# Moving u*B to GpSimd in 152 of 576 scan steps of a bidirectional Mamba kernel

## The reference

```
xz = u @ W_in; x, z = split(xz); x = silu(conv(x) + b)
dt, B, C = split(x @ W_x);  delta = softplus(dt @ W_dt + b_dt);  A = -exp(A_log)
h[d, n] = exp(delta[d] * A[d, n]) * h[d, n] + delta[d] * x[d] * B[n]      # over time
y[d]    = sum over n of h[d, n] * C[n]
out     = ((y + x * D) * silu(z)) @ W_out
```

## Time and profile before

| what | value |
|---|---|
| median of 3 runs | 2344.05 us (2339.93 to 2344.3) |
| the profiled execution's own time | 2339.7 us |
| its span | 2337.9 us |
| DVE busy | 2127.7 us (91%) |
| PE busy | 1875.8 us (80%) |
| POOL busy | 1613.1 us (69%) |
| ACT busy | 1147.4 us (49%) |

### The profile page before, as it was taken

One profiled execution on the slowest core, in us unless ns is written; L12 is line 12 of the kernel. 1 busy time (PEld: TensorE's weight loads), 2 busy tenths in 40 slices (PEclk: granted clock), 3 DMA queues, 4 the chain that ended last, 5 costly groups with the idle time before them and its releaser, 6 DMA issues. The chain is left out here.

```text
span 2337.9 us, 15732 instructions
## 1 busy us (share of the span) xinstructions
PE 1875.8 (80%) x4794; PEld 723.8 (31%) x4794; DVE 2127.7 (91%) x1429; ACT 1147.4 (49%) x1316; POOL 1613.1 (69%) x704
## 2 busy tenths in 40 slices
PE   5698879787798788788779779869778978877676
PEld 2233333232233233233233323323323323222222
DVE  2899999778999998998999998999899999899996
ACT  3647464644646444534655544644474553353331
POOL 0767875745876884775796686687487678478665
PEclk8899999899999999999999999999999999999999
DMA  3335434333544544443453453454344454345443
GB/s 100 121 139 131 148 141 130 109 104 130 142 144 145 143 145 128 141 149 110 146 159 138 143 152 129 146 142 146 109 140 146 143 143 145 113 151 153 146 149 87
DMA packets 96159, 317.20 MB, mean 136 GB/s; under 512 B 14588, under 2 KB 18956, under 8 KB 95948
## 3 DMA queue, kind: packets, MB, share of 16 engines
q1 hardware_dynamic: 96076, 316.21, 43.2%
HBM read 307.31 MB, written 4.72 MB: 133 GB/s over the span
## 5 line engine op out<-in xcount | busy, mean ns | idle before, releaser
L823 POOL TENSOR_TENSOR ring<-ring,c_ring 128x1024 f32<-128x1024 f32 x576 | 1353.3, 2356 | 644.4 <-DVE ring L769 643.6
L769 DVE TENSOR_TENSOR_SCAN ring<-a_ring,b_ps 128x1024 f32<-128x1024 f32 x576 | 1314.9, 2283 | 37.7 <-issue 0.9
L453 PE MATMUL y_ps<-ring,wp 128*128 128x512 f32 x2304 | 1182.7, 615 | 58.5 <-DVE yv_rows L755 25.6
L453 PEld LDWEIGHTS y_ps<-ring,wp 128*128 128x128 f32 x2304 | 441.6, 196 | 460.1 <-issue 323.7
L573 ACT ACTIVATE a_ring<-delta_ab,neg_a 128x1024 f32<-128x1024 f32 x384 | 435.1, 1144 | 264.1 <-DVE ring L769 258.6
L741 DVE TENSOR_TENSOR b_ps<-u_ab,b_ps 128x1024 f32<-128x1024 f32 x384 | 464.5, 1210 | 102.8 <-PE b_ps L445 79.0
L445 PE MATMUL b_ps<-b_in,sel 96*128 96x512 bf16 x768 | 238.5, 393 | 146.8 <-DVE ring L769 146.5
L573 ACT ACTIVATE a_ring<-delta_m,neg_a 128x1024 f32<-128x1024 f32 x192 | 219.3, 1147 | 265.5 <-DVE ring L769 265.5
L445 PE MATMUL b_ps<-b_in,sel_m 96*128 96x512 bf16 x384 | 119.8, 394 | 148.4 <-DVE ring L769 148.4
L741 DVE TENSOR_TENSOR b_ps<-u_m,b_ps 128x1024 f32<-128x1024 f32 x192 | 232.0, 1208 | 5.0 <-PE b_ps L445 4.7
L500 PE MATMUL bank<-x,w_conv 96*128 96x512 f32 (+12 forms) x576 | 207.2, 602 | 8.3 <-DVE xs L785 8.3
(11 more groups left out here) (82 smaller groups left out, 1095.9 us busy)
## 6 DMA issues: line engine op xcount, KB each, us to landing
c_ring<-c_rows SPq DMA_DIRECT2D x384, 512.0 KB, 3.7
c_ring<-c_rows SPq DMA_DIRECT2D x384, 256.0 KB, 3.9
out<-io SPq DMA_DIRECT2D x16, 192.0 KB, 2.2
io<-x SPq DMA_DIRECT2D x6, 384.0 KB, 4.7
b_in<-parts SPq DMA_DIRECT2D x36, 64.0 KB, 2.1
dt_in<-parts SPq DMA_DIRECT2D x72, 24.0 KB
c_rows<-c_out SPq DMA_DIRECT2D x24, 64.0 KB, 3.2
wp<-wpack SPq DMA_DIRECT2D x1, 1185.0 KB
```

The source lines that it names most:

```text
L453: nc.tensor.matmul(half(y_ps[:, :], j), ident, half(ring[:, g % RING, :], j), start=(n == 0), stop=(n == NS - 1)).then_inc(g_summed, 1)
L769: nc.vector.tensor_tensor_scan(out=h, data0=a, data1=b, initial=0.0, op0=ALU.mult, op1=ALU.add).then_inc(h_ready, 1)
L823: nc.gpsimd.tensor_tensor(r, r, c_ring[:, g % C_RING, :], ALU.mult).then_inc(g_ready, 1)
```

## The change

`BY_POOL` names steps within an item: 11 in `rows`, 13 in `fwd`, 14 in `bwd`, which gives 4 x 38 = 152 steps. In these steps PE spreads no B row and DVE makes no product. SP instead fetches the row B[n] from DRAM, broadcast to 128 partitions, into the new `b_ring` (2 slots in SBUF), up to six steps ahead, and POOL multiplies it in place by u, three steps ahead. The scan of such a step reads a from `a_ring` and b from `b_ring`. ACT's copy that cut out the C rows now takes the B rows too, and SP stores both to DRAM. The slots of `b_ps` go round over the 424 other steps. Smaller packed weights make room for `b_ring`; the products made with them have the same sizes. `ring` keeps its five slots.

```diff
+B_RING = 2
+B_LEAD = 6
+BY_POOL = {ROWS: (2, 8, 13, 17, 19, 23, 26, 30, 31, 37, 47),
+           FWD: (3, 7, 9, 11, 13, 15, 16, 17, 20, 25, 27, 31, 42),
+           BWD: (5, 7, 10, 11, 15, 16, 19, 21, 23, 27, 31, 33, 41, 43)}
-SP_ORDER = ("ahead_c", "jobs")
+SP_ORDER = ("ahead_b", "ahead_c", "jobs")
+POOL_ORDER = ("ahead_b", "product", "jobs")
...
+            def spread_row(dst, rows, k, n, landed_in):
+                if k < 2:
+                    sp.dma_start(dst, rows[k, n:n + 1, :].to_broadcast([P, T])).then_inc(landed_in, 16)
+                    return
+                for b in range(2):
+                    sp.dma_start(dst[b * DM:(b + 1) * DM, :],
+                                 rows[b, n:n + 1, :].to_broadcast([DM, T])).then_inc(landed_in, 16)
...
+            def look_ahead_b(g):
+                if g >= ALL_STEPS:
+                    return
+                kind, pair, k, n = step_at(g)
+                if g % STEPS == 0:
+                    sp.wait_ge(c_kept, 64 * (g // STEPS + 1))
+                if by_pool[g]:
+                    m = pool_before[g]
+                    if m >= B_RING:
+                        sp.wait_ge(h_ready, pool_steps[m - B_RING] + 1)
+                    spread_row(b_ring[:, b_slot(g), :], b_rows[parity(kind, pair)], k, n, b_spread[b_slot(g)])
...
-                wait(pe, h_ready, g - 1)
+                if by_pool[g]:
+                    return
+                m = dve_before[g]
+                if m >= 2:
+                    pe.wait_ge(h_ready, dve_steps[m - 2] + 1)
...
             def scan(g):
...
+                if by_pool[g]:
+                    dve.wait_ge(b_made, pool_before[g] + 1)
+                    b = b_ring[:, b_slot(g), :]
+                else:
+                    dve.wait_ge(b_used, dve_before[g] + 1)
+                    b = b_ps[:, p_slot(g), :]
...
+            def look_ahead(g):
+                if g >= ALL_STEPS or not by_pool[g]:
+                    return
+                kind, pair, k, n = step_at(g)
+                pool.wait_ge(K["set_ready"][kind], 3 * pair + nth(k))
+                pool.wait_ge(b_spread[b_slot(g)], b_uses[g])
+                b = b_ring[:, b_slot(g), :]
+                nc.gpsimd.tensor_tensor(b, u_of(kind, pair, k), b, ALU.mult).then_inc(b_made, 1)
```

More of the change, by code:

```diff
@@ L1 @@
+import itertools
 import numpy as np
@@ L295, in build_program @@
         unit_of = {j[:4]: j[4] for p in PARTS for slot in p["slots"] for j in slot}
+        by_pool = [g % STEPS in BY_POOL[ITEMS[g // STEPS]["kind"]] for g in range(ALL_STEPS)]
+        pool_steps = [g for g in range(ALL_STEPS) if by_pool[g]]
+        dve_steps = [g for g in range(ALL_STEPS) if not by_pool[g]]
+        pool_before = list(itertools.accumulate([0] + [int(x) for x in by_pool]))
+        dve_before = [g - n for g, n in enumerate(pool_before)]
+        dmas = lambda g: 2 if g % STEPS // NS == 2 else 1
         c_uses, spread = [], [0] * C_RING
         for g in range(ALL_STEPS):
-            spread[g % C_RING] += 2 if g % STEPS // NS == 2 else 1
+            spread[g % C_RING] += dmas(g)
             c_uses.append(16 * spread[g % C_RING])
+        b_uses, spread = {}, [0] * B_RING
+        for m, g in enumerate(pool_steps):
+            spread[m % B_RING] += dmas(g)
+            b_uses[g] = 16 * spread[m % B_RING]
+        b_slot = lambda g: pool_before[g] % B_RING
+        p_slot = lambda g: dve_before[g] % 2
         use_of = {j[:4]: j[5] for p in PARTS for slot in p["slots"] for j in slot}
@@ L337, in step_at, with walk @@
             return it["kind"], it["pair"], s // NS, s % NS
-        def walk(order, job, **phases):
+        def walk(order, job, LEAD=LEAD, **phases):
             for n, part in enumerate(PARTS):
@@ L442, in look_ahead @@
                     pe.wait_ge(K["bc_loaded"][kind], BC_LOADS * (pair + 1))
-                wait(pe, h_ready, g - 1)
+                if by_pool[g]:
[3 more added lines that the diff above has]
+                    pe.wait_ge(h_ready, dve_steps[m - 2] + 1)
                 for j in range(2):
-                    last = nc.tensor.matmul(half(b_ps[:, g % 2, :], j), pick(k, n), half(b_in[:, parity(kind, pair), :], j), start=True, stop=True)
+                    last = nc.tensor.matmul(half(b_ps[:, p_slot(g), :], j), pick(k, n), half(b_in[:, parity(kind, pair), :], j), start=True, stop=True)
                 last.then_inc(b_ready, 1)
@@ L525, in job @@
                     src = source(kind, pair)
-                    w = by_batch("w_z", layer, C)
+                    w = col("w_z", layer)[0:C, :]
                     if k < 2:
-                        product(unit, P, [(w[0], half(src[:, k, :], j))])
+                        product(unit, P, [(w[:, 0:P], half(src[:, k, :], j))])
                     else:
-                        product(unit, P, [(w[1 + b], half(src[:, b, :], j)) for b in range(2)])
+                        room(unit)
+                        for b in range(2):
+                            last = nc.tensor.matmul(bank[b * DM:(b + 1) * DM, unit % 2, :], w[:, P:DI], half(src[:, b, :], j),
+                                                    start=True, stop=True)
+                        last.then_inc(produced[unit % 2], 1)
                 elif name == "constants":
@@ L545, in job @@
                     pe.wait_ge(gated_done[kind], 3 * (pair + 1))
-                    w = by_batch("w_out", layer)
-                    product(unit, C, [(w[0], half(yv_of(kind, pair, k), j)), (w[1 + k], half(yv_of(kind, pair, 2), j))])
+                    w, own = col("w_out", layer), slice(k * DM, (k + 1) * DM)
+                    product(unit, C, [(w[:, 0:C], half(yv_of(kind, pair, k), j)),
+                                      (w[own, C:2 * C], half(yv_of(kind, pair, 2), j)[own, :])])
                 elif name == "centre":
@@ L628, in job @@
                     src = full(unit)
-                    if k < 2:
-                        wait(act, b_used, STEPS * (ordinal[kind, pair] - 1) + NS * (k + 1))
+                    if k < 2 and ordinal[kind, pair]:
+                        upto = STEPS * (ordinal[kind, pair] - 1) + NS * (k + 1)
+                        act.wait_ge(b_used, dve_before[upto])
+                        wait(act, b_made, pool_before[upto])
                     bias = sm[:, m_of(k), 5:6]
@@ L850, in tile_of @@
                 return TILES * ordinal[kind, pair]
-            walk(("product", "jobs"), job, product=product)
+            walk(POOL_ORDER, job, ahead_b=look_ahead, product=product)
 def pack(inputs):
```

61 lines of the change are left out of this document (29 added, 32 removed).

## The result

The changed kernel takes 2485.11 us (median of 4 runs, 2481.93 to 2488.66) against 2342.81 us before (4 runs, 2339.93 to 2344.3). The ratio is 1.061, with a 95% interval of 1.0591 to 1.0628: 6% slower, where 5% was forecast.

The account below looks back on a forecast made before the run. DVE was taken to set the pace, with PE as busy in fwd and bwd steps 0 to 17. Forecast: 2339.7 + 85 - 34 + 33 + 30 = 2454, rounded to 2455 us, 5% slower; range 2330 to 2590.

Parts of the forecast that it names:

- The scan waits for POOL: In the 152 moved steps, a scan with two SBUF inputs stands still until the running POOL product has ended.
- POOL waits for the scan: In moved steps, POOL is held while the scan reads two SBUF inputs, taken as 2.09 us per scan.
- The sum by stretch: Per stretch of an item, the longer of POOL's need and the shortened old length: +85 us, corrected by -34.
- the two further waits: Scans meeting a running product in DVE-paced stretches, 33 us, and POOL standing for B rows in fwd, 30 us.
- The waits at DVE's pace: In stretches left to DVE's pace, a scan waits on average half of a running POOL product: 33 us.
- POOL keeps what it holds: Rival: queued POOL products pass a waiting scan, 5 to 7 us on a third of 152; 2585 us or more; 5%.
- my case: Main forecast: moved scans and POOL products exclude each other, the second comer waiting; slower, 2361 to 2585 us, 77%.
- SP's late B rows: In fwd, B rows of steps 16 and 17 delay queued C rows; POOL stands 3.7 us twice per item, 30 us.
- DVE alone waiting: Rival: POOL runs on while a moved scan reads, only DVE waits; 2266 to 2364 us, 10%.
- no contention at all: Rival: moved scans slip between POOL's reads and keep 2.28 us; about 2190 us, faster; 7%.
- The signs named beforehand: Expected in the later profile: scan and POOL product durations, POOL's busy share, DVE's idle waits, middle windows near 60 us.

Follow-up runs that it names:

- The fifth experiment: The changed kernel with 20 of the 152 moved steps given back to PE and DVE: 2415.61 us, ratio to before 1.031.
- the third experiment: The changed kernel, but in the 152 steps ACT writes a to PSUM and the scan reads b from b_ring: 2236.6 us, ratio to before 0.955.

## Why the prediction was right, and which terms were off

**The scan waits for POOL.** Right, and shown by both directions of test: taking the second SBUF operand away takes 250 us off, adding it alone costs 131 us. The row of L800 was enough to read it.

**POOL waits for the scan.** Right: the value 2.09 us was chosen without a row, and the trace shows 2.15 us for the scan's own part, with products held for one DVE instruction and once for four. POOL was held 205 us in all, not 152 x 2.09 = 318: only 93 of its instructions were held by about 2 us, the others met no such scan.

**The sum by stretch.** This is the term with the wrong sizes. It says +10.1 for bwd (10.9 measured), +10.4 for fwd (15.4) and +0.7 for rows (11.9). Inside the items it is off more: the middle stretches (fwd, bwd, rows) were to grow by 7.3, 6.9 and 6.5 us and changed by -4.2, +4.5 and +1.1, while the heads were to change by +4.3, -0.3 and -4.8 and changed by +12.3, +3.1 and +8.7, and the tails by -1.2, +3.5 and -1.0 and changed by +7.3, +3.4 and +2.1. Two things explain part of it. I counted a u*B product in the stretch of its step, but it stands three steps ahead; and the POOL jobs of slot 31 run at the edge, so they fall to the tail: the stretches of fwd 1 have 32, 17 and 29 POOL instructions, where I counted 29, 22 and 23. The head of rows holds the 11-us scan of step 2, which the sum had no term for. Over the twelve items, this sum (+51) and the two further waits (33 and 30) came to +114 us, and 140 were measured; by the sum alone the four `rows` were to change by 3 us and the four fwd by 12, and they changed by 59 and 37. That 2455 lies only 30 us from 2485 is therefore in part luck: stretches forecast too long offset stretches forecast too short.

**The waits at DVE's pace.** 33 us, as if a scan met the rest of one product. It was too small. The rival "POOL keeps what it holds", at 5%, is how the long scans come about, though on some 25 of the 152 and not on a third; most of the others came in at the end of the running product, as my case had it. The fifth experiment puts 70 us on 20 steps.

**SP's late B rows.** 30 us taken, within 0 to 60. POOL stood 14.5 us for them in the changed kernel and 54 us once nothing else held it [group L889 of the third experiment]. The mechanism is there; it is mostly covered here.

**The rivals on the other side.** DVE alone waiting is ruled out by POOL's durations, no contention at all by 3947 against 2283 ns. What the second would have brought, 2190 us, is 46 us below the time with one operand in PSUM, 2236.

**The signs named beforehand.** Scans from PSUM at 2.28 us: yes. POOL's product mean over 2.6: yes, 2.65, but with its maximum at 9.2 instead of 4.5. DVE idle for b: yes, 11.5 us; for `g_summed`, no row. Missed: the mean of the moved scans, 3.95 us instead of 3 to 3.5; POOL over 90% busy, 88%; the middle windows of bwd and rows near 60 us, 57.5 and 54.5.

Open: how much of the loss in the heads, where PE shares the pace, comes from PE itself. The granted clock in the head of fwd 1 is 0.87 where it was 0.96, and the y_ps matmuls take 665 ns on average, 631 in the third experiment. Over the program PE has 119 us less to do and is busy for 58 us longer (1934.1 against 1875.8). No run holds its clock apart from the waits. Open too: why POOL passes a waiting scan in some meetings and not in others that look the same.

## What to carry to other kernels

Before giving DVE's work to POOL, look at where DVE's operands end up, not only at how much POOL has to spare: an instruction that reads PSUM and SBUF and one that reads SBUF twice have the same duration alone and not beside a busy POOL. One slow instance of a similar instruction in the trace (maximum twice the median, its end tied to another engine's end) is enough to expect the halts. It does not give their number: the moved scans took 3.95 us where 3 to 3.5 was expected. And if a buffer in PSUM becomes free by the change, put the other operand there: that turned 6% slower into 4.5% faster with the same distribution of work.

## What the runs showed of the hardware that was not expected

A waiting instruction doesn't always get its turn when the other engine's current one ends. A scan waited for the POOL product that ran and for three more behind it (1486.45 to 1495.73 us, scan 11.06 us long), and a product waited for four DVE instructions (9.17 us). But in some 83 meetings the scan came in at the end of the running product, with POOL's next one ready.

A held instruction is recorded as busy from its start, so DVE was busy for 89 us longer with 184 us less to do, and POOL for 205 us more than its added work. The durations by form show it.
